# Three single moves in a hand-written table of slots: a norm piece and score pieces of the second attention

## The reference

```python
q, k, v = heads(x @ Wq), heads(x @ Wk), heads(x @ Wv)
k, v = concat([mem_k, k]), concat([mem_v, v])
q, k = l2norm(q), l2norm(k)                     # each row by its own norm
dots = einsum('bhid,bhjd->bhij', q, k) * 10.0
dots = einsum('hg,bgij->bhij', W_pre_th, dots)  # mixes the heads
dots = where(causal, mask_value, dots)
vk = top_k(dots, 64)[0][..., -1:]
dots = where(dots < vk, mask_value, dots)       # keeps the 64 largest
attn = einsum('hg,bgij->bhij', W_post_th, softmax(dots))
out = einsum('bhij,bhjd->bhid', attn, v) * head_scale
out = (out * sigmoid(x @ Wg + bg)) @ Wo
```

## Time and profile before

| | us |
|---|---|
| median of 3 runs | 3034.32 (3026.36 to 3034.89) |
| profiled execution | 3030.27 |
| its span, first to last instruction | 3028.2 |

### The profile page before, as it was taken

How to read it: one execution, slowest core, us unless ns; L and a number is a source line. 1 busy time by engine, 2 the same in 40 slices (tenths; PEclk the granted TensorE clock), 3 DMA queues, 4 the chain that set the end, 5 groups by cost and what they waited for, 6 DMA issues and landing times. The chain is left out here.

```text
span 3028.2 us, 58900 instructions
## 1 busy us (share of the span) xinstructions
PE 2561.9 (85%) x18372; PEld 1570.0 (52%) x18372; DVE 2319.0 (77%) x7745; ACT 2025.6 (67%) x5415; POOL 1305.6 (43%) x3717
## 2 busy tenths in 40 slices
PE   4799999999887888888888888888888888776998
PEld 1233444334345655565565565565555565565565
DVE  4656666664349979979989898898998998994664
ACT  1366655565368878878878878887887787773331
POOL 2212222211025656656656655665655665673000
PEclk6799999999989999999999999999999999986999
DMA  2111111001021121121212112112112112111532
GB/s 103 43 33 40 44 44 40 30 19 52 11 53 31 39 52 36 41 46 40 43 32 50 40 24 65 37 26 61 36 33 56 32 37 57 31 40 46 119 89 60
DMA packets 111292, 137.01 MB, mean 45 GB/s; under 512 B 20448, under 2 KB 90592, under 8 KB 110464
## 3 DMA queue, kind: packets, MB, share of 16 engines
q1 hardware_dynamic: 109968, 132.00, 18.1%
q10 hardware_dynamic: 1008, 1.18, 0.1%
HBM read 47.56 MB, written 13.24 MB: 20 GB/s over the span
## 5 line engine op out<-in xcount | busy, mean ns | idle before, releaser
L1299 ACT ACTIVATE junk<-xs,thr 128x420 bf16<-128x420 f32 (+12 forms) x832 | 465.3, 568 | 70.6 <-POOL thr L1000 55.6
L1134 PE MATMUL pt<-wsc,attn 128*128 128x128 f32 x2560 | 359.7, 289 | 98.0 <-POOL wsc L981 62.6
L1119 PE MATMUL pm<-mixin,pre_b 128*128 128x258 f32 (+15 forms) x1088 | 361.3, 447 | 90.9 <-ACT xs L1292 80.0
L1134 PEld LDWEIGHTS pt<-wsc,attn 128*128 128x128 f32 x2560 | 322.5, 198 | 190.7 <-POOL wsc L981 131.4
L1421 DVE MAX8 best<-left 128x8 f32<-128x420 f32 (+12 forms) x832 | 368.9, 484 | 0.0
L1085 PE MATMUL pa<-kT,qT 64*128 64x258 f32 (+3 forms) x1248 | 273.3, 443 | 85.7 <-ACT arena L1261 59.0
L1261 ACT ACTIVATE arena<-pa,nrm 128x258 f32<-128x258 f32 (+3 forms) x624 | 266.6, 480 | 82.8 <-PE pa L1085 76.9
L1451 DVE SCALAR_TENSOR_TENSOR attn<-xs,bound,ex 128x420 f32<-128x420 f32 (+14 forms) x480 | 226.5, 500 | 119.5 <-issue 57.9
L1119 PEld LDWEIGHTS pm<-mixin,pre_b 128*128 128x128 f32 x1088 | 175.0, 198 | 223.7 <-issue 192.4
L1318 ACT COPY at<-pt 128x128 f32<-128x128 f32 (+3 forms) x512 | 198.2, 450 | 116.3 <-PE po L1172 96.3
L1308 ACT ACTIVATE ex<-xs,negm 128x228 f32<-128x228 f32 (+15 forms) x512 | 239.0, 518 | 0.1
(11 more groups left out here) (264 smaller groups left out, 5885.7 us busy)
## 6 DMA issues: line engine op xcount, KB each, us to landing
spread<-gates_dram SPq DMA_DIRECT2D x32, 512.0 KB, 8.2
mixin<-arena SPq DMA_DIRECT2D x32, 258.0 KB
mixin<-arena SPq DMA_DIRECT2D x32, 242.0 KB
mixin<-arena SPq DMA_DIRECT2D x32, 226.0 KB
mixin<-arena SPq DMA_DIRECT2D x32, 210.0 KB
mixin<-arena SPq DMA_DIRECT2D x32, 194.0 KB
q_stack<-parts_dram SPq DMA_DIRECT2D x96, 64.0 KB
parts_dram<-parts SPq DMA_DIRECT2D x15, 384.0 KB, 2.3
```

Source lines behind the costliest of these rows:

```text
L1119: ins = nc.tensor.matmul(bank[:, 0:jn], pre_b[:, :], mixin[:, m % MIX_SLOTS, j0:j0 + jn], start=True, stop=not last)
L1134: ins = nc.tensor.matmul(bank[:, P * k:P * k + P], attn[:, m % A_SLOTS, P * k:P * k + P], wsc[:, m % A_SLOTS], start=True, stop=True)
L1299: ins = nc.scalar.activation(junk[:, z, 0:width(n)], xs[:, m % X_SLOTS, 0:width(n)], ACT.Sign, scale=-1.0, bias=thr[:, s % LIVE, z:z + 1], ...
```

## The change

Three entries of the table of slots are edited; no instruction is added or removed. Pieces are dealt to the letters in their order, so adding a letter early and taking one late moves every piece between the two places by one letter.

```diff
-                put(before, at((10, "AA"), (11, "B"), (12, "B"), (13, "AC"), (14, "BC")), "ns", b)
+                put(before, at((10, "AA"), (11, "AB"), (12, "B"), (13, "C"), (14, "BC")), "ns", b)
...
-                put(before, at((23, "C"), (24, "ABBC"), (25, "AB"), (26, "AAB"), (27, "BBB"), (29, "ABB")), "qk3", b)
-                put(now, at((1, "ABC"), (2, "AB"), (3, "AB"), (4, "A")), "qk1", b)
+                put(before, at((23, "C"), (24, "ABBC"), (25, "AB"), (26, "AABB"), (27, "BBB"), (29, "AB")), "qk3", b)
+                put(now, at((1, "C"), (2, "ABC"), (3, "ABC"), (4, "A")), "qk1", b)
```

## The result

The changed kernel takes 3091.0 us (median of 4 runs, 3087.0 to 3102.3), the kernel before beside it 3031.5 us (3026.4 to 3034.9): the ratio is 1.0185, 95% interval 1.0161 to 1.021. It is slower, as forecast, but by 59.5 us where 20 were forecast, and 3091 lies above the stated range of 3032 to 3066. It is 72 us longer than the profiled one of the kernel before: 5.5 us stand ahead of the first row maximum (873.2 against 867.7 us; no run ties them to the change), and the eight turns are longer by 7.9, then four times 10.2 to 10.3, then 6.8, 8.3 and 2.6 us.

The account below looks back on a forecast made before the run. No engine is full; a turn (238.89 us) is a chain of waits passing between engines. The terms 20.3 + 6.8 - 7.0 = +20.1 us on 3030.3 gave 3050.4, stated as 3051, range 3032 to 3066.

Parts of the forecast that it names:

- A rule to weigh: TensorE's full clock needs recent activity, so the new wait of about 2 us in step 11 speaks against the change.
- rival B: Step 11's new wait drops the clock under the TensorE run behind it: 1.7 us a turn, 12 more, 3063; chance 0.12.
- The sum: The three edits' waits added over their turns: 20.3 + 6.8 - 7.0 = +20.1 us, giving 3051; chance 0.53.
- Part 3: Fourth tile's score piece moves from 29B to 26B: 0.5 saved twice, -1.0 us a turn, seven turns -7.0.
- Part 1: Third norm piece moves to 11A: ScalarE 3.28 us late, 0.4 returned; +2.9 a turn, seven turns +20.3.
- the 4.2 at the attention: VectorE's wait at the attention of step 11 would be near 4.2 us instead of 0.98.
- the 0.4 given back: Of the 1.10 us of squares that leave step 13 on ScalarE, 0.4 us a turn gets through.
- Rival D: Step 12's 3.66 us wait swallows step 11's 3.28 whole; norm edit worth -0.4 a turn, total 3028; chance 0.07.
- Part 2: Second tile's score pieces move later, steps 1 to 4: -0.95 + 0.75 + 0.3 + 0.75 = +0.85 us a turn, eight turns +6.8.
- The head start: Two score pieces leaving step 1's way to the exponentials bring about 0.95 us earlier arrival, then spent by later pieces.
- Rival C: Step 1's head start survives: 0.95 us a turn gained instead of 0.85 lost, 14 less, 3037; chance 0.10.
- Rival E: Half-clock stretches fall elsewhere, off the chain: 1.46 us a turn, 10 less, 3041; chance 0.08.

Follow-up runs that it names:

- e1_ns: The norm-piece edit alone, put into the kernel before: 3062.2 us, ratio 1.009.
- e10_base: The kernel before, no edits, plus the second set of fillers (useless TensorE matmuls, more at steps 2 and 16, none at steps 0 and 1): 3022.5 us, ratio 0.9965.
- e8_warm_qk1: The kernel before with only the second-tile score edit, plus the first set of fillers (useless TensorE matmuls at ten places): 3046.4 us, ratio 1.0039.
- e6_warm_all: The changed kernel (all three edits) plus the first set of fillers, useless TensorE matmuls at ten places: 3040.4 us, ratio 1.0014 to the kernel before.
- e4_fill: The changed kernel plus sixteen useless TensorE matmuls ahead of the waiting tail product in step 11: 3059.3 us, ratio 1.0075 to the kernel before.
- e2_qk1: The second-tile score edit alone, put into the kernel before: 3073.0 us, ratio 1.0134.
- e9_best: The kernel before with only the fourth-tile score edit (29B to 26B), plus the second set of fillers: 3011.9 us, ratio 0.9928.
- e7_warm_qk3: The kernel before with only the fourth-tile score edit (29B to 26B), plus the first set of fillers at ten places: 3014.5 us, ratio 0.9932.
- e11_all: The changed kernel (all three edits) plus the second set of fillers: 3056.0 us, ratio 1.0068 to the kernel before.

## Why the prediction was right in direction and wrong in size

**The failed step** is "A rule to weigh" and rival B that it led to. The sum compared waits at a fixed clock: it took for granted that the four stretches at 1.2 GHz of a turn stay where they are and put the clock at nothing. Outside the sum, rival B priced it at one place only, the norm pair behind the new wait: 1.7 us a turn, with a chance of 0.12. What the runs show in its place, per turn:

- the waits: 239.2 - 236.5 = +2.7 us (forecast +2.75; 2.1 to 3.5 by the other pairs);
- half clock: 238.9 - 236.5 = 2.4 us in the kernel before, 249.2 - 239.2 = 10.0 us after; +7.6 us.

Together +10.3, which is 249.2 - 238.9. Over seven turns the waits are 19 us. The other 40 of the 59.5 are put down to the clock as what is left: the turns were profiled in one execution of each kernel, 72 us apart, and not in the median ones.

The condition of rival B failed as well. It tied the clock to the new wait in step 11, and e1_ns has that wait at full clock, while part 3, which moves nothing at steps 1 and 5, brought new stretches there.

**Part 1** (forecast +2.9): +3.26 in step 11 and -0.43 in step 14, +2.8. The 2.2 us wait, its releaser, the 4.2 at the attention, the 2.5 left of step 12 and the 0.4 given back were all seen. Rival D, that step 12 swallows it, is refuted. Not foreseen was how far the clock's part in step 11 would reach: not 1.7 but 13.47 - 10.95 = 2.5 us, with scores (2.66 us for 1.92) as well as the norm pair.

**Part 2** (forecast +0.85): against e10_base, e8_warm_qk1 has -1.13 in step 1, +0.83 in step 2, +0.62 in step 3, +0.04 in step 4 and +1.06 in step 5: +1.4; e6_warm_all +1.3, with 9.00 in step 3. Both turns have a stretch at 1.2 GHz from step 2 into step 3, so this is not the waits alone. In the sixth turn of e4_fill (from 2090.01), whose stretch ends 2.8 us into step 2, steps 1 to 5 take 5.22, 9.78, 8.51, 9.53 and 9.80 us, 0.75 more than in e10_base. The forecast lies between these; how much waits are worth without any such stretch, no run shows. The head start at step 1 was right, and that it is lost again. It is lost in part at a place that the estimate left out: it stopped at the copies ahead of step 4 and took VectorE's 0.19 in step 5 for the place where the sum arrives. In step 5 e8_warm_qk1 has two waits instead, and e4_fill one:

```profile
1399.26 0.67 DVE L1375 BATCH_NORM_STATS2 moments<-xs 128x6 f32<-128x484 f32 x1 [0.40 <-ACT xs L1308]
...
1400.67 0.67 DVE L1375 BATCH_NORM_STATS2 moments<-xs 128x6 f32<-128x484 f32 x1 [0.74 <-ACT xs L1308]
```

```profile
2138.38 0.66 DVE L1363 BATCH_NORM_STATS2 moments<-xs 128x6 f32<-128x484 f32 x1 [0.70 <-ACT xs L1296]
```

Rival C, that the head start survives, is refuted. The clock's part is larger: e2_qk1 cost 40 us, of which at most 1.4 x 8 = 11 are these waits.

**Part 3** (forecast -1.0): -0.70 in step 29 and -0.48 in step 0, -1.2. In e9_best 0.44 comes back in step 27. It takes the piece at 26B and the second fillers together: e7_warm_qk3 and e6_warm_all, with the piece and the first fillers, have 5.67 us there, and e10_base, with the second fillers and without the piece, 5.66; which of the fillers it is, no run tells. Right as a wait, and wrong in sign as a time, 17.5 us slower, until the clock was held up.

**Other readings.** The prediction said that eight turns repeat almost to the tenth; only the second to sixth do (238.9 to 239.0 us), the first and seventh take 237.3 and 237.5, and the last is shorter. Rival E thought of stretches that fall elsewhere, but only as a gain, off the chain. They did fall elsewhere, and there were more of them: 307 us for 157.

The rule of the Trainium skill that I weighed (TensorE: Matmul & The Clock Gate, Part 1) spoke the right way for the changed kernel: behind the new wait of 2.23 us the granted clock is 0.50. In e1_ns it is 1.00 behind the same wait, so the rule alone doesn't give the price. A second one of the same page ("HAM oscillation — how this bites in real kernels") prices such time at half of what is spent at the lower clock. The seven stretches of the turn after are some 37 us long, so it would make 19 us of them; 10.0 were measured, against a turn that has one such stretch itself. Some stretches delay nobody, as those of steps 2 and 16 before. So the trace does not agree with that rule as a price of the turn; here it is too high.

**Still open.** Why the stretches fall in steps 2, 14, 16 and 27 before, and what makes every second turn of e11_all differ, no run settles. Ahead of the stretches of steps 2, 14 and 16 in the kernel before TensorE had been busy 1.28 of 3.0, 1.67 of 3.2 and 1.03 of 3.1 us:

```profile
1600.30:1603.30 3.00, 1.28 (x4) 0.69 (x5) 2.91 (x12) 3.00 (x9) 1.03 (x6) 1.00 0.33 67
1695.70:1698.90 3.20, 1.67 (x10) 1.10 (x10) 3.17 (x14) 3.03 (x11) 1.71 (x6) 1.00 0.38 77
1719.70:1722.80 3.10, 1.03 (x5) 0.85 (x6) 2.17 (x11) 3.09 (x9) 1.35 (x6) 1.00 0.00 0
```

and in step 11 after, 1.69 of 3.2 us. The same 3.2 us of e1_ns, laid around the tail's product in the same way, have the same 1.69, and there the clock does not fall. So what TensorE did just ahead does not decide it alone. First the changed kernel, then e1_ns:

```profile
1713.20:1716.40 3.20, 1.69 (x11) 1.13 (x11) 3.20 (x10) 2.34 (x8) 1.39 (x5) 1.00 0.00 0
```

```profile
1695.75:1698.95 3.20, 1.69 (x11) 1.12 (x11) 3.20 (x10) 2.34 (x8) 1.39 (x5) 1.00 0.00 0
```

A third buffer for the squares, which would take away the 2.19 us wait itself, was not tried.

## What to carry to other kernels

Before pricing a shift of a microsecond in a kernel whose TensorE is busy 85% of the time with a granted clock under 1, list the stretches at the lower clock and what each costs on the chain. Then open the range on that side: any shift can move them, also at steps that it does not touch, and each may cost nothing or up to the work in it at half speed. To separate waits from clock, fill TensorE's idle times with matmuls of no use in both kernels and compare single turns at full clock, and more than one pair of them. A gain that is seen at its place and missing in the time (part 3) is not a wrong idea yet: look whether the clock took it.

## What was not expected of the hardware

Matmuls that compute nothing made a kernel 1.6% faster (3091.0 to 3040.4 us), and even the tuned one 0.35% (e10_base). TensorE's clock fell to 1.2 GHz behind single waits of 2.2 us (step 11 after) and even of 0.54 us (step 14 before, with one of 1.24 ahead of it), and behind the same wait of 2.23 us it fell in the changed kernel and stayed up in e1_ns. And the same instructions in the same order took 240.0 us in one turn and 244.8 in the next.
